# Attention's weights leave the start of a two-expert-stage kernel, and its first routing works in groups of 2, 2, 4, 4 and 4 tiles

## What is computed

```python
x = x + 0.5 * ffn(layernorm(x), gate, w0, w1, wo_ffn)
x = x + attn(layernorm(x), wq_a, qn_w, wq_b, wkv_a, kvn_w, wkv_b, wo)
x = x + 0.5 * ffn(layernorm(x), gate, w0, w1, wo_ffn)
# ffn: top 2 of x @ gate, softmax over the two, then
#   sum over the chosen e of p_e * ((silu(x @ w0[e]) * (x @ w1[e])) @ wo_ffn[e])
# attn: q = rms_norm(x @ wq_a, qn_w) @ wq_b      -> per head 64 plain + 64 rotated columns
#   latent, k_pe = split(x @ wkv_a)              -> 64 + 64 columns
#   kv = rms_norm(latent, kvn_w) @ wkv_b         -> per head 64 key + 64 value columns
#   softmax(q k^T / sqrt(128)) v, all heads, then @ wo
```

## Time and profile before

| | us |
|---|---|
| median of 3 runs | 1102.12 (1101.56 to 1106.17) |
| the profiled execution | 1114.29 |
| its span, first to last instruction | 1112.2 |
| before the first expert tile on PE | 79.5 |
| first expert stage on PE | 79.5 to 277.5 |
| attention | 277.5 to about 802 |
| output projection with the second routing | 802 to 883 |
| tables and empty rows, until the second stage's first tile | 883 to 898.4 |
| second expert stage, to the end | 898.4 to 1112.2 |

### The profile page before, as it was taken

The page is one execution under the profiler, slowest core; times in us unless marked ns, Lnnn a source line. Parts: engine busy times, 40 slices in busy tenths (PEclk is TensorE's granted clock), DMA queues, the critical chain, the costliest instruction groups (busy, mean ns, idle before and its releaser), DMA issues. The chain is left out here.

```text
span 1112.2 us, 22773 instructions
## 1 busy us (share of the span) xinstructions
PE 1038.3 (93%) x6286; PEld 820.7 (74%) x6287; DVE 723.6 (65%) x1647; ACT 523.5 (47%) x1139; POOL 477.1 (43%) x418
## 2 busy tenths in 40 slices
PE   4669999999779999999999999999999989999993
PEld 4658888887447777777778777777789658888883
DVE  5364666654367878878887788888556836665552
ACT  2243433422056766776766677677411224433321
POOL 2552344443344553647454644443125503344432
PEclk9999999999889999999999999999999899999998
DMA  9843544432200111101111101111567435544330
GB/s 243 270 158 91 133 105 104 108 52 38 58 0 11 58 39 39 39 20 39 40 39 39 38 23 37 40 39 39 191 203 256 155 113 125 142 105 104 52 50 11
DMA packets 71615, 95.87 MB, mean 86 GB/s; under 512 B 9616, under 2 KB 48656, under 8 KB 71312
## 3 DMA queue, kind: packets, MB, share of 16 engines
q1 hardware_dynamic: 57232, 78.04, 22.5%
q0 software_dynamic: 14304, 16.87, 8.9%
HBM read 64.37 MB, written 34.43 MB: 89 GB/s over the span
## 5 line engine op out<-in xcount | busy, mean ns | idle before, releaser
L868 ACT ACTIVATE shared<-bank,small 128x512 f32<-128x512 f32 x256 | 176.5, 690 | 92.6 <-DVE small L1323 91.7
L1323 DVE TENSOR_REDUCE small<-bank 128x1 f32<-128x512 f32 x256 | 174.7, 685 | 44.3 <-PE bank L1696 44.1
L1706 PE MATMUL bank<-constants,shared 128*128 128x128 f32 x1024 | 156.6, 276 | 2.4 <-ACT shared L877 1.2
L804 ACT CAST split_rows_and_inner<-bank 128x512 fp32r<-128x512 f32 x78 | 45.8, 587 | 238.8 <-PE bank L1493 238.8
L1706 PEld LDWEIGHTS bank<-constants,shared 128*128 128x128 f32 x1024 | 122.9, 141 | 44.9 <-issue 14.1
L1510 PE MATMUL bank<-expert_weights_low,split_rows_and_inner 128*128 x312 | 143.3, 459 | 0.0
L1512 PE MATMUL bank<-expert_weights_high,split_rows_and_inner 128*128 x312 | 142.6, 457 | 0.0
L1508 PE MATMUL bank<-expert_weights_high,split_rows_and_inner 128*128 x312 | 125.5, 402 | 2.9 <-DVE split_rows_and_inner L1109 2.5
L1694 PE MATMUL bank<-expert_weights_high,shared_split 128*128 128x512 f32 x256 | 123.0, 480 | 1.4 <-POOL shared_split L608 1.4
L1114 DVE TENSOR_TENSOR split_rows_and_inner<-bank,split_rows_and_inner 128x512 fp32r<-128x512 f32 x78 | 53.9, 691 | 107.4 <-ACT split_rows_and_inner L804 107.2
L599 POOL TENSOR_TENSOR shared<-shared 128x512 f32<-128x512 f32 x32 | 41.3, 1290 | 190.0 <-DVE shared L1333 190.0
(11 more groups left out here) (195 smaller groups left out, 2222.7 us busy)
## 6 DMA issues: line engine op xcount, KB each, us to landing
expert_weights<-L_ffn_w_kernel SPq DMA_DIRECT2D x32, 512.0 KB, 5.0
shared<-rows_by_expert SPq DMA_DIRECT2D x78, 129.0 KB, 2.1
expert_weights<-L_ffn_wo_kernel SPq DMA_DIRECT2D x16, 512.0 KB, 6.6
shared<-inverse_sums SPq DMA_DIRECT2D x64, 128.0 KB, 2.9
attended_transposed<-shared SPq DMA_DIRECT2D x32, 256.0 KB, 3.0
expert_weights<-attended_transposed SPq DMA_DIRECT2D x2, 2048.0 KB, 10.1
shared<-attended_transposed SPq DMA_DIRECT2D x2, 2048.0 KB, 10.3
rows_by_expert<-empty_rows SPq DMA_DIRECT2D x23, 129.0 KB, 3.1
```

Source lines behind the costliest of these rows:

```text
L868: nc.scalar.activation(prob[k % 4], bank[k % 4][:, :], ACT.Exp, bias=negmax[:, k % 8:k % 8 + 1], accum_out=psum[par][:, hh * GT + qt:hh * ...
L1323: V.tensor_reduce(negmax[:, k % 8:k % 8 + 1], bank[k % 4][:, :], AX.X, ALU.max, negate=True).then_inc(max_ready, 1)
L1706: last = tr(bank[4 + k % 2][:, c * P:(c + 1) * P], prob[k % 4][:, c * P:(c + 1) * P], ident)
```

## The change

1. SP loads only the first part of the constants, then two tiles of the input, then the rest. The other constants and all of attention's weights are loaded inside the first expert stage: seven DMAs at its tile 2, five at tile 3, one at tile 37. The head weights come from arrays that are laid out by head before the launch, so that they need no transposes on the chip.
2. The folding (query with key weights, value with output weights, the rotated part's layout) stands behind `moe(0)` on every engine; the folding of values takes the place of `keep_busy(5, 7)`.
3. The first routing works in groups of 2, 2, 4, 4, 4 tiles. Each group has its own rows (`rows0`) and its own row numbers, so that no group waits for scatters. GpSimd's list still has all roots first.
4. Masks, carried sums and the constant matrices of `ranks` are kept as float32r, in both routings.
5. The empty rows of the first stage are written by SP (four DMAs) and ACT (four). Those of the second stage are replaced by 32 DMAs during attention that fill the whole table (544 rows of 1032 bytes each, 561 KB a DMA); GpSimd waits for them before the second routing's scatters.
6. `keep_busy(14, 4)` ahead of the second stage becomes `keep_busy(10, 4)`.

```diff
-GN = (GT, 2)
+GROUPS = (((0, 2), (2, 2), (4, GT), (8, GT), (12, GT)), tuple((2 * g, 2) for g in range(NT // 2)))
+GN = 2
...
+TAGS = 8
...
+VALUE_BANKS = (7, 0, 1, 7)
...
+        rows0 = area(o, [NT, TOPK, ROW])
+        rope_w = area(o, [PAIRS, 2, ROPE])
+        qnT, knT, vT = (area(o + (k + 1) * NH * HD, [NH, HD], HD) for k in range(3))
+        stage_o = area(o + 4 * NH * HD, [NH, D], HD)
...
         @block.sync
         def _(sp):
-            sp.dma_start(cst[:, :], const).then_inc(const_in, 16)
+            first = x_in[0].rearrange("(t p) d -> p t d", p=P)
+            sp.dma_start(cst[:, 0:C_KCOS], const[:, 0:C_KCOS]).then_inc(const_in, 16)
+            sp.dma_start(xall[:, 0:GN, :], first[:, 0:GN, :]).then_inc(x_in_sem[0], 16)
             sp.dma_start(ids[:, :], ids_in).then_inc(const_in, 16)
             sp.dma_start(gate_sb[:, :, :], gate.rearrange("(c p) e -> p c e", p=P)).then_inc(const_in, 16)
-            for g in range(NG):
+            sp.dma_start(xall[:, GN:GT, :], first[:, GN:GT, :]).then_inc(x_rest_in, 16)
+            for g in range(1, NG):
                 sp.dma_start(xall[:, g * GT:(g + 1) * GT, :],
                              x_in[g].rearrange("(t p) d -> p t d", p=P)).then_inc(x_in_sem[g], 16)
-            sp.dma_start(wproj[:, :, 0:2 * HD], wkv_a.rearrange("(c p) n -> p c n", p=P)).then_inc(attw_in, 16)
-            sp.dma_start(wproj[:, :, 2 * HD:3 * HD], wq_a.rearrange("(c p) n -> p c n", p=P)).then_inc(attw_in, 16)
-            sp.dma_start(norm_w[0:HD, 1:2], kvn_w.rearrange("(p a) -> p a", a=1)).then_inc(attw_in, 16)
-            for k in range(2):
-                sp.dma_start(norm_w[k * HD:(k + 1) * HD, 0:1], qn_w.rearrange("(p a) -> p a", a=1)).then_inc(attw_in, 16)
-                sp.dma_start(stage_q[k * HD:(k + 1) * HD], wq_b).then_inc(attw_in, 16)
-            sp.dma_start(stage_kv, wkv_b).then_inc(attw_in, 16)
-            sp.dma_start(stage_o, wo.rearrange("(h v) n -> v h n", v=HD)).then_inc(attw_in, 16)
+
+            def load_tables():
+
+                sp.dma_start(cst[:, C_KCOS:C_ALL], const[:, C_KCOS:C_ALL]).then_inc(const_in, 16)
+                sp.dma_start(wproj[:, :, 0:2 * HD], wkv_a.rearrange("(c p) n -> p c n", p=P)).then_inc(attw_in, 16)
+                sp.dma_start(wproj[:, :, 2 * HD:3 * HD], wq_a.rearrange("(c p) n -> p c n", p=P)).then_inc(attw_in, 16)
+                for k in range(2):
+                    rows_ = slice(k * HD, (k + 1) * HD)
+                    sp.dma_start(norm_w[rows_, 0:1], qn_w.rearrange("(p a) -> p a", a=1)).then_inc(attw_in, 16)
+                    sp.dma_start(norm_w[rows_, 1:2], kvn_w.rearrange("(p a) -> p a", a=1)).then_inc(attw_in, 16)
+                sp.dma_start(kvn_row[:, :], kvn_w.rearrange("(a n) -> a n", a=1).to_broadcast([HD, HD])).then_inc(attw_in, 16)
+
+            def load_head_weights():
+
+                for k in range(2):
+                    sp.dma_start(rope_w[k * HD:(k + 1) * HD].rearrange("p a h n -> p (a h n)"), wq_rope).then_inc(attw_in, 16)
+                for to, w in ((qnT, wq_in), (knT, wk_in), (vT, wv_in)):
+                    sp.dma_start(to.rearrange("p h n -> p (h n)"), w).then_inc(attw_in, 16)
+
+            def load_output_weights():
+
+                sp.dma_start(stage_o, wo.rearrange("(h v) n -> v h n", v=HD)).then_inc(attw_in, 16)
...
-                sp.wait_ge(tables_ready[f], 1)
-                for e in range(E):
-                    n = sp.value_load(cnt_i[0:1, e:e + 1], min_val=0, max_val=T)
-                    sp.dma_start(xs[bass.ds(n + e * REGION, P), :], zrow[:, :]).then_inc(tails_zeroed[f], 16)
-                sp.wait_ge(tails_zeroed[f], 16 * (E if f else E + SPARE))
-                for u in range(3):
-                    sp.wait_ge(scattered[f][u], 16 * GN[f] * TOPK * ((NT // GN[f] + 2 - u) // 3))
+                if f == 0:
+                    sp.wait_ge(tables_ready[f], 1)
+                    for e in range(E // 2):
+                        n = sp.value_load(cnt_i[0:1, e:e + 1], min_val=0, max_val=T)
+                        sp.dma_start(xs[bass.ds(n + e * REGION, P), :], zrow[:, :]).then_inc(tails_zeroed[f], 16)
+                    sp.wait_ge(tails_zeroed[f], 16 * (E + SPARE))
+                    sp.wait_ge(scattered[0][0], 16 * NT * TOPK)
+                else:
+                    for u in range(3):
+                        sp.wait_ge(scattered[1][u], 16 * GN * TOPK * ((NT // GN + 2 - u) // 3))
...
+                    if f == 0 and among(t, 2):
+                        load_tables()
+                    if f == 0 and among(t, 3):
+                        load_head_weights()
+                    if f == 0 and among(t, TILES - 2):
+                        load_output_weights()
...
+            def empty_rows(p):
+
+                n = E * REGION // NPAIR
+                sp.dma_start(xs[p * n:(p + 1) * n, :].rearrange("(p k) c -> p k c", k=TAGS),
+                             zrow[0:n // TAGS, :].unsqueeze(1).to_broadcast([n // TAGS, TAGS, ROW])).then_inc(tails_zeroed[1], 16)
...
+            for p in range(4):
+                empty_rows(p)
             for p in range(NPAIR - 4):
                 store(p, p % 2)
                 spread(p + 2, p % 2)
+                empty_rows(p + 4)
 
...
-            for g in range(NG):
+            for g, (t, n) in enumerate(GROUPS[0]):
                 pool.wait_ge(veps_ready[0], g + 1)
-                root(0, g * GT, GT)
-            for g in range(NG):
+                root(0, t, n)
+            for g in range(len(GROUPS[0])):
                 scatter(0, g)
             pool.wait_ge(xd_copied, 16)
...
+            pool.wait_ge(const_in, 64)
+            root_first(0)
+            root_first(1)
             pool.wait_ge(folded_w, 2)
             pool.wait_ge(wa_ready, 1)
             load_weights(0, 0)
-            root_first(0)
-            root_first(1)
             root_rows(1)
...
+            pool.wait_ge(tails_zeroed[1], 16 * NPAIR)
+            for g in range(NT // GN):
...
+            act.wait_ge(tables_ready[0], 1)
+            for e in range(E // 2, E):
+                n = act.value_load(cnt_i[0:1, e:e + 1], min_val=0, max_val=T)
+                nc.scalar.dma_start(xs[bass.ds(n + e * REGION, P), :], zrow[:, :]).then_inc(tails_zeroed[0], 16)
...
-            for k in range(2):
-
-                act.wait_ge(fold_psum, 6 + k + 1)
-                src = bank[6 + k][:, :].rearrange("p (a h n) -> p a h n", a=4, h=2)
-                for hh in range(2):
-                    last = nc.scalar.copy(wpair[:, 4 * k:4 * k + 4, 2, (1 - hh) * HD:(2 - hh) * HD], src[:, :, hh, :])
-                last.then_inc(folded_w, 1)
-                split_high(0, 0, k)
-            for k in range(4):
-                act.wait_ge(fold_psum, 8 + k + 1)
-                nc.scalar.copy(wvo[:, 2 * k:2 * k + 2, :].rearrange("p a n -> p (a n)"), bank[k][:, :]).then_inc(folded_w, 1)
-                split_high(0, (2 + k) // 3, (2 + k) % 3)
+            for e in range(2):
+                for piece in range(3):
+                    split_high(0, e, piece)
...
+            act.wait_ge(attw_in, 16 * 13)
+            act.wait_ge(scaled_w, 1)
+            for k in range(2):
+
+                act.wait_ge(fold_psum, k + 1)
+                src = bank[4 + k][:, :].rearrange("p (a h n) -> p a h n", a=4, h=2)
+                for hh in range(2):
+                    last = nc.scalar.activation(wpair[:, 4 * k:4 * k + 4, 2, (1 - hh) * HD:(2 - hh) * HD], src[:, :, hh, :],
+                                                ACT.Copy, scale=norm_w[:, 0:1])
+                last.then_inc(folded_w, 1)
+
+            def value_weights(k, b):
+
+                act.wait_ge(fold_psum, 2 + k + 1)
+                nc.scalar.activation(wvo[:, 2 * k:2 * k + 2, :].rearrange("p a n -> p (a n)"), bank[b][:, :],
+                                     ACT.Copy, scale=norm_w[:, 1:2]).then_inc(folded_v, 1)
+
             rows_out(0, 0, 0)
...
+            def first_stats(g):
+                t, n = GROUPS[0][g]
+                dve.wait_ge(x_rest_in if g == 1 else x_in_sem[t // GT], 16)
+                ln_stats(xall[:, t:t + n, :], t, n, veps_ready[0])
+
+            def norm_first(g):
+                t, n = GROUPS[0][g]
+                dve.wait_ge(rstd_ready[0], g + 1)
+                ln_rows(0, g, xall[:, t:t + n, :], t)
+
+            groups = len(GROUPS[0])
             own.step(V.memset(zero8, 0.0))
+            first_stats(0)
             dve.wait_ge(const_in, 48)
-            def first_stats(g):
-                dve.wait_ge(x_in_sem[g], 16)
-                ln_stats(xall[:, g * GT:(g + 1) * GT, :], g * GT, GT, veps_ready[0])
-
-            def norm_first(g):
-                dve.wait_ge(rstd_ready[0], g + 1)
-                norm_rows(0, g, xall[:, g * GT:(g + 1) * GT, :])
-
-            first_stats(0)
+            own.step(V.tensor_copy(rank_ops[:, 0:2 * P], cst[:, C_UP:C_UP + 2 * P]))
+            own.step(V.tensor_scalar(carry, iota_e, 0.0, None, ALU.mult))
```

(60 more changed lines are left out.)

200 lines of the change are left out of this document (86 added, 114 removed).

## The result

The kernel after takes 1110.30 us (median of 20, 1105.75 to 1115.78); the kernel before, run beside it, takes 1104.83 (20 runs, 1100.13 to 1113.59). The ratio is 1.0038, 95% interval 1.002 to 1.0056: slower by 0.4% (the two medians are 0.5% apart), 21.6 us above the forecast of 1088.7 and 13.3 above the upper end of its range. 2.7 of the 21.6 are the starting point: the forecast was counted from 1102.12, the median of three runs.

The account below looks back on a forecast made before the run. PE bounds the middle of attention and the expert stages, so gains lie in stretches where PE has little to do. Terms -6.2 + 0.4 - 2.7 - 4.9 = -13.4 from the median 1102.12 give 1088.7 us, range 1082.5 to 1097.

Parts of the forecast that it names:

- term 1: Start, up to the first expert tile: last scatter ends earlier, -6.2 us, bounds -1.5 and -11.
- loads inside the first stage: First expert stage: the moved weight loads still let rows reach PE in time, 0 us, bounds 0 and +4.
- term 2: Behind the first expert stage: folding fits waits or replaces idle matmuls, +0.4 us, bounds 0 and +3.5.
- Term 3: Second routing: float32r halves the ranks' matmul records, 0.37 us a group, -2.7 us, bounds 0 and -4.
- Term 4: Second stage's start: without empty rows the first tile follows the last scatter by 4.67 us, -4.9, bounds -3 and -5.5.
- Attention, 0: Attention's 32 pairs: each 561 KB write lies behind the pair's loads and costs nothing, 0 us.
- The rival "slower": Attention: empty-row writes end up ahead of the sums' loads in 28 pairs, 2.2 us each, 1150 us; chance 0.05.
- GpSimd stands still for all 7.1 us: Start: DVE's low parts of the experts' weights block GpSimd throughout, 3.9 us more, 1092.6; chance 0.12.
- the fourth rival: Start: GpSimd runs dry between groups, or loads in the expert stage hold PE 4 us, 1097.4; chance 0.08.

Follow-up runs that it names:

- after_again: The kernel after, unedited, run again beside the kernel before on another chip: 1112.9 us, ratio 1.0072.
- less_busy: The kernel before with keep_busy(8) in place of keep_busy(12) behind the first expert stage: 1105.9 us, ratio 1.0007.
- spaced: The kernel after with all 32 empty-row writes kept but none ahead of the first pair's store, four pairs having two: 1108.4 us, ratio 0.9951.
- writes_alone: The kernel before with the 32 writes during attention, first four in a burst, and without the eight behind the second tables: 1123.9 us, ratio 1.0081.
- load_alone: The kernel before with one extra, unneeded 1 MB load of output weights at tile 37 of the first expert stage: 1120.6 us, ratio 1.0066.
- late_only: The kernel after with only the output weights' load moved behind the first two loads of attention's rows: 1112.3 us, ratio 0.9992.
- late_output: reorder with the output weights' load moved from tile 37 to behind the first two loads of attention's rows: 1095.8 us, ratio 0.9909.
- late_split: late_output with the second stage's eight empty-row writes shared by SP and ACT, four each: 1099.7 us, ratio 0.9901.
- early_tables: late_output with tile 2's eight loads moved back to the start, behind the first two experts' weights: 1098.4 us, ratio 0.9933.
- again: The kernel before, unedited, profiled once more: 1116.0 us, one run, beside the kernel before's 1114.5.
- undo_writes: The kernel after without the writes during attention, the eight empty-row writes behind the second tables restored: 1111.8 us, ratio 0.9969.
- ranks32: late_output with the ranks' masks, sums and constant matrices kept as fp32 in both routings: 1103.3 us, ratio 0.9917.
- undo_busy: undo_writes with keep_busy(9) in place of keep_busy(3) ahead of attention's first rows: 1105.4 us, ratio 0.9984.
- reorder: undo_writes with the first group's scatters ahead of the fifth root in GpSimd's list: 1100.1 us, ratio 0.9944.

## Why the prediction was wrong

Its terms beside the stretches of after_again less those of less_busy (same call; less_busy differs from before by four idle matmuls and no measurable time). The spans are 1102.6 and 1113.6, 11.0 apart, where the medians are 6.9 apart, so single rows can be off by some us:

| | predicted | measured |
|---|---|---|
| start (term 1) | -6.2 | -10.1 |
| loads inside the first stage, until its last add | 0 | +8.1 |
| folding (term 2), to the scores | +0.4 | +0.4 |
| pairs 1 to 4 | 0 | +1.5 |
| pairs, the burst | 0 | +13.7 |
| second routing (terms 3 and 4) | -7.6 | -4.3 |
| second stage | 0 | +1.5 |
| sum | -13.4 | +10.8 |

- **Attention, 0: the step that failed most.** "The write stands behind the pair's loads and ahead of a store that nobody awaits for a pair's time" was true of the single writes (spaced). But the first four writes stand together, and the step priced their bytes and landing, not the time in which SP can issue nothing else. Behind them stood not only a store but the third pair's sums, then GpSimd's list, then PE. The rival "slower" had the right place, SP's queue ahead of the sums, and a wrong form: it charged 28 pairs, where one place pays 11 to 14 us once. writes_alone, with the burst and nothing else of the change but the missing eight writes, is 9.0 us slower than the kernel before.
- **Loads inside the first stage, 0, bounds 0 and +4: the second.** I asked whether rows reach PE in time, and they do ("stage" 190 to 192 throughout). The chain that ends the stage is another one, GpSimd's adds, and the load at tile 37 meets it where little can be made good. load_alone puts it at 7.3 us (4.2 to 10.5), its trace at 2 to 3, and late_only and late_output at about 4. The bound of +4 was not far off, its reason was. Of the +8.1 in the table the load is some 3 to 4 us; the rest is slower adds of this profile, which come and go without it (late_split has 12.4, the first profile of before 12.9). The loads at tile 2 are eight, not seven, and cost nothing that early_tables could show.
- **Term 1, -6.2:** right in mechanism in the first pair of profiles, too small: 8.7. The first scatter starts at 23.75, 1.5 earlier than worked out, and the low parts cost two scatters 1.0 each and not three: 2.0 instead of 3.2. The rival "GpSimd stands still for all 7.1 us" falls: DVE works 6.90 us, GpSimd loses 2.0. The Trainium skill (SBUF — State Buffer, "SBUF: two separate sides") has the loser of the shared ports block for a whole instruction, and two scatters that are 1.0 us longer beside instructions of 1.2 us agree with that; the prediction's reading that it must be so for all six in a row does not hold here. A premise was wrong for other executions: "The folding of weights ... was beside this wait too and brings nothing by leaving". In again, writes_alone and load_alone the folding ends behind the last scatter and holds the first tile, and there the new start is worth 14 to 15 us without the reordering. In the same calls GpSimd also runs dry once, 4.7 to 4.8 us ahead of the seventeenth scatter (undo_writes, spaced, late_only), which the fourth rival had.
- **Term 2, +0.4:** right in its parts: the value folding's 32 records took 3.67 us, where I had 3.5, and the heads' folding lay in DVE's wait. That the whole stretch came out at +0.4 is partly luck, since it is 29.4 to 32.1 in profiles of the kernel before. The +1.5 of pairs 1 to 4 is 3.4 us at the lower clock, which less_busy doesn't have there.
- **Term 3, -2.7:** mis-sized; half the records are not half the time. A group's ranks take 0.59 instead of 0.74 us, 0.15 and not 0.37, about 1.2 us in eight groups; ranks32 gives 1.4, which is no more than the profiles vary.
- **Term 4, -4.9:** the first tile does follow the last scatter by 4.97 us (4.67 forecast), but terms 3 and 4 together bring 3.3 to 4.3 of 7.6, and writes_alone, without the eight writes and with the ranks as before, 2.8. In undo_writes, with the eight writes back, the stretch is 96.5 and still 0.6 to 2 under before's.
- **The clock** is 0.006 to 0.012 lower in every kernel with the new start. The prediction had only +0.3 for it. Idle matmuls don't explain it (undo_busy, less_busy). Part of it is a trace of the waits, such as the 13.7 us at the lower level that follow the burst's stall in after_again; part has a price, as pairs 1 to 4 show. How much of the loss it makes stays open, as does the spread of undo_writes.

What the change was worth without its two faults, by the two calls that can be compared: 1.0072 as it is, 0.9944 without the writes during attention and with the reordering (reorder), 0.9909 with the later load as well (late_output), 0.9% faster than the kernel before. late_split's 0.9901 holds some 0.005 of before's late start and doesn't show that it is better.

## What to carry to other kernels

A transfer put "behind" the urgent ones must be priced by what its queue can't do while it is issued, and by the first place where several stand together, not by the average pair. Before loads are moved into a busy stage, find the chain that ends it (here adds that wait for each other's landing, 4.6 us of every 4.88), and see how late in it they stand: early delays are made good, late ones hardly are. One part added alone to the kernel before settles a cause that traces of different executions only suggest (writes_alone). And ratios from different calls can be compared only if the kernel before behaves alike in both: here its start differed by 10 us, more than most effects that were sought.

## What the runs showed of the hardware

- The issue time of SP's DMAs grows when several large writes stand together. One write of 561 KB (548.2 in the page's unit) in rows of 1032 bytes takes 0.73 us to issue, two take 3.89, four 18.4, and a 256 KB store behind one of them 3.0 to 3.6 instead of 0.58 (writes_alone: 18.09 for four). The Trainium skill (Perfetto Trace Analysis, "DMA Instruction — HWDGE (DVE, Sync)") says that the window shown spans the generation of descriptors, and that engines start before its end when more are generated than the buffer holds; it has no figure for this case, and that SP is held because such a buffer is full is a guess that fits the 18.44 us and that no run shows.
- A 1 MB load by SP delays an add that GpSimd issues beside it: its wait for the add before it is 5.65 and 6.30 us in two profiles instead of 3.1, and 3.47 in another. The Trainium skill (DMA: Bandwidth & Descriptors, "Queues, rings and completion order") lets each engine take packets in turn from the queues it has work for, so that another queue gives no shelter; the longer waits agree.
- The same kernel has two starts: the kernel before needs 81.4 us to its first hidden matmul in one profile and 93.3 in another, and its later stretches agree within a few us. It isn't the chip: on B less_busy has 83.6 and load_alone 93.1. In the late ones ACT stands still for 13.92 us ahead of the folding with no releaser to be seen; the reason is open.
